# Loading the router's context a second time with its inner dimensions exchanged, in a transformer block with a routed expert layer

## The reference

```python
nx = _layer_norm(x, ln_gamma, ln_beta)
q = nx @ Wq
k = prototype_bank @ Wk            # prototype_bank is the context
v = prototype_bank @ Wv
scores = jnp.einsum('bth,bph->btp', q, k) * H ** (-0.5)
weights = jax.nn.softmax(scores, axis=-1)
evidence = jnp.einsum('btp,bph->bth', weights, v)
combined = jnp.concatenate([nx, evidence, anchor], axis=-1)
router_probs = jax.nn.softmax(combined @ router_W + router_b, axis=-1)
h = jax.nn.silu(jnp.einsum('btc,ecr->bter', combined, e_w1) + e_b1)
expert_out = jnp.einsum('bter,erh->bteh', h, e_w2) + e_b2
routed = jnp.sum(expert_out * router_probs[..., None], axis=-2)
g = jax.nn.sigmoid(jax.nn.silu(combined @ gate_w1 + gate_b1) @ gate_w2 + gate_b2)
return x + g * (routed @ out_w + out_b)
```

## Time and profile before

| | |
|---|---|
| median of 3 runs | 570.68 us (568.03 to 572.41) |
| span of the profiled execution | 569.2 us |
| TensorE busy (matmuls) | 536.2 us, 94% |
| VectorE busy | 433.4 us, 76% |
| ScalarE busy | 384.8 us, 68% |
| POOL busy | 276.2 us, 49% |

### The profile page before, as it was taken

The page is one execution under the profiler, slowest core; times in us unless marked ns, Lnnn a source line. Parts: engine busy times, 40 slices in busy tenths (PEclk is TensorE's granted clock), DMA queues, the critical chain, the costliest instruction groups (busy, mean ns, idle before and its releaser), DMA issues.

```text
span 569.2 us, 16513 instructions
## 1 busy us (share of the span) xinstructions
PE 536.2 (94%) x6209; PEld 388.2 (68%) x6209; DVE 433.4 (76%) x1271; ACT 384.8 (68%) x897; POOL 276.2 (49%) x296
## 2 busy tenths in 40 slices
PE   6988999899999999999999889998999999999995
PEld 5745666566656666666667566655888788788895
DVE  4778889788989889898877577865586686786565
ACT  6536778687777787877877575564764864864862
POOL 5637849579497787888840422224224124124100
PEclk9989999899999999999999899999999999999999
DMA  4765635534154352453410010000000000000000
GB/s 131 159 172 132 178 101 159 123 95 112 51 133 119 96 134 68 113 134 82 125 32 5 1 37 1 1 1 18 20 20 20 28 24 24 19 20 18 18 20 18
DMA packets 48716, 39.38 MB, mean 69 GB/s; under 512 B 6241, under 2 KB 48002, under 8 KB 48642
## 3 DMA queue, kind: packets, MB, share of 16 engines
q1 hardware_dynamic: 46568, 34.62, 23.2%
q10 hardware_dynamic: 2074, 3.77, 2.4%
HBM read 10.06 MB, written 2.10 MB: 21 GB/s over the span
## 4 chain that ended last, share of the span: by engine, by line
PE 64%; DVE 13%; POOL 7%; DMA 5%; issue 4%; ACT 4%; SPq 2%; ACTq 0%; DVEq 0%; POOLq 0%
PE PS L959 31%; PE PS L1837 7%; PE PS L1803 6%; PE PS L1889 4%; PE PS L995 3%; PE PS L1901 3%; DMA Qs<-MT 2%; PE PS L1821 2%; DVE NM L1617 2%; PE PS L1859 2%; PE PS L1894 2%; SPq L1347 2%; DVE r_T L934 2%; DVE r_R L937 1%; PE PS L1881 1%
## 5 line engine op out<-in xcount | busy, mean ns | idle before, releaser
L1617 DVE TENSOR_REDUCE NM<-PS 128x4 f32<-128x512 f32 x256 | 163.3, 681 | 30.1 <-PE PS L1803 29.5
L1503 ACT ACTIVATE PR<-PS 128x512 f32<-128x512 f32 x256 | 139.7, 599 | 27.2 <-PE PS L1821 26.6
L1803 PEld LDWEIGHTS PS<-Ks,Qs 64*128 64x128 bf16 x1024 | 57.7, 95 | 53.8 <-DVE NM L1617 29.6
L1803 PE MATMUL PS<-Ks,Qs 64*128 64x128 bf16 x1024 | 83.8, 219 | 5.2 <-DVE NM L1617 3.8
L1821 PE MATMUL PS<-Qs,Ks 64*128 64x128 bf16 x1024 | 84.2, 220 | 4.1 <-DMA Qs<-MT 3.5
L1837 PE MATMUL PS<-PR,Va 128*32 128x128 f32 x2048 | 84.2, 283 | 0.0
L742 ACT ACTIVATE r_HID<-PS,ANC 128x128 f32<-128x128 f32 x224 | 63.0, 381 | 19.4 <-PE PS L959 19.4
L653 POOL TENSOR_TENSOR m_veps<-m_mv,m_eps 128x4 f32<-128x4 f32 x16 | 3.6, 224 | 132.6 <-DVE m_mv L821 132.6
L1837 PEld LDWEIGHTS PS<-PR,Va 128*32 128x32 f32 x2048 | 49.0, 110 | 20.9 <-ACT PR L1503 6.5
L1821 PEld LDWEIGHTS PS<-Qs,Ks 64*128 64x128 bf16 x1024 | 57.5, 95 | 7.9 <-DMA Qs<-MT 4.0
L959 PE MATMUL PS<-r_NXS,r_WNS 128*128 128x512 f32 x168 | 53.2, 424 | 0.0
(11 more groups left out here) (201 smaller groups left out, 1121.2 us busy)
## 6 DMA issues: line engine op xcount, KB each, us to landing
Qs<-Qp SPq DMA_DIRECT2D x96, 128.0 KB
Ks<-Kp SPq DMA_DIRECT2D x90, 128.0 KB
CTXG<-in_ctx SPq DMA_DIRECT2D x8, 256.0 KB, 3.8
r_CTX<-in_ctx SPq DMA_DIRECT2D x8, 256.0 KB, 2.8
out<-X SPq DMA_DIRECT2D x8, 256.0 KB, 2.3
X<-in_x SPq DMA_DIRECT2D x7, 256.0 KB, 4.3
W<-in_weights ACTq DMA_DIRECT2D x2, 855.0 KB
Qs<-MT SPq DMA_DIRECT2D x62, 8.0 KB
```

The lines of the kernel that those rows point to most:

```text
L1503: nc.scalar.activation(PR[:, u, :], T_BANK[u % 2][:, :], ACT.Exp, scale=SCALE)\
L1617: nc.vector.tensor_reduce(out=NM[:, c.b // 2, c.second, u // 2, u % 2 * 4:u % 2 * 4 + 4, 0], in_=S_BANK[score_bank(c, u)[0]][:, :].rearran ...
L1803: last = nc.tensor.matmul(S_BANK[bank][:, j * P:(j + 1) * P], Qs[c.stack][rows, lo + j, cols], Ks[c.stack][rows, lo + j, cols], start=True ...
```

## The change

The host hands over one more array, the context with its last two dimensions exchanged. SP loads it into `CTXT` right behind the load of `CTX`, for the same group and on the same semaphore, which so counts 32 a load. As `CTXT` has one buffer, SP first waits until the keys product of the group before is done. The step `ctx_turn` goes from the lists, from TensorE and from ScalarE, and `keys` on TensorE waits for the loads and for `nx_read`. As the lists are shorter by one, the slices in `rest_of_groups` change, and with them how steps are spread there.

```diff
 ROUTER_STEPS = (
     ("probs", 0, 0), ("weigh", 1, 0),
-    ("hidden", 0, 0), ("ctx_turn", 2, 0),
+    ("hidden", 0, 0),
     ("hidden", 0, 1), ("stats", 2, 0),
...
-    for i, b in ((NG - 3, lead[0:3]), (NG - 2, lead[3:]), (NG - 1, second[:-2])):
+    for i, b in ((NG - 3, lead[0:2]), (NG - 2, lead[2:]), (NG - 1, second[:-2])):
...
-    ctx_turned = sem("ctx_turned")
-    ctx_read = sem("ctx_read")
...
                 sp.dma_start(CTX[par][:, :, :], ctxin[bass.ds(g * GB, GB)].rearrange("b p h -> p b h"))\
                     .then_inc(ctx_in[par], 16)
+                if later(g):
+                    sp.wait_ge(keys_done, g)
+                sp.dma_start(CTXT[:, :].rearrange("h (b p) -> h b p", b=GB),
+                             ctxtin[bass.ds(g * GB, GB)].rearrange("b h p -> h b p")).then_inc(ctx_in[par], 16)
...
-            elif name == "ctx_turn":
-                act.wait_ge(ctx_turned, g + 1)
-                nc.scalar.activation(CTXT[:, :], EVIDENCE_BANK[:, :], ACT.Copy).then_inc(ctx_read, 1)
...
-            if name == "ctx_turn":
-                pe.wait_ge(ctx_in[par], 16 * (pair + 1))
+            if name == "keys":
+                pe.wait_ge(ctx_in[par], 32 * (pair + 1))
                 if later(g):
                     pe.wait_ge(nx_read, g)
-                turn(EVIDENCE_BANK, lambda b: CTX[par][:, b, :]).then_inc(ctx_turned, 1)
-            elif name == "keys":
-                pe.wait_ge(ctx_read, g + 1)
                 product(EVIDENCE_BANK[:, :], A[:, :], CTXT[:, :]).then_inc(keys_done, 1)
...
+        "ctxt": np.ascontiguousarray(a["ctx_1024"].transpose(0, 2, 1)),
```

More of the change, by code:

```diff
@@ L457, in later, with mlp_and_router @@
     return not isinstance(g, int) or g > 0
-def mlp_and_router(nc, stack, X, V, ctxin, w, vec, rows1, condT, mod, gbm, half, zeros, YT, ident, PS, load_w2, out,
+def mlp_and_router(nc, stack, X, V, ctxin, ctxtin, w, vec, rows1, condT, mod, gbm, half, zeros, YT, ident, PS, load_w2, out,
                    bank_filled, bank_read, shifted_done, max_done, exp_done, o_normed, o_stored,
@@ L1127, in mlp_and_router, with build_block @@
     return sync_programs, gpsimd_programs, scalar_programs, vector_programs, tensor_programs
-def build_block(nc, xin, cond, ctxin, weights, vectors, ident_in, rowb, out):
+def build_block(nc, xin, cond, ctxin, weights, vectors, ident_in, rowb, ctxtin, out):
     stack = ExitStack()
@@ L1217, in build_block @@
         sync_programs, gpsimd_programs, scalar_programs, vector_programs, tensor_programs = mlp_and_router(
-            nc, stack, X, V, ctxin, w, vec, rows1, condT, mod, gbm, half, zeros, YT, ident, PS, load_w2, out,
+            nc, stack, X, V, ctxin, ctxtin, w, vec, rows1, condT, mod, gbm, half, zeros, YT, ident, PS, load_w2, out,
             bank_filled, bank_read, shifted_done, max_done, exp_done, o_normed, o_stored, high_ready, low_ready)
```

## The result

The changed kernel takes 562.53 us (median of 4 runs, 561.32 to 564.71), the kernel before 569.97 us in the same comparison (4 runs, 568.03 to 572.41). The ratio is 0.9884, with a 95% interval from 0.9848 to 0.9919: faster by 4.6 to 8.7 us. The forecast was 564.8 us, a ratio of 0.9897 against the 570.68 us then shown. The profiled span fell from 569.2 to 561.2 us.

A forecast was written before the change was run, and what follows sets the result against it. TensorE was taken to bound the router, busy 164.3 of 171.2 us. The terms 0.44 + 1.7 + 0.45 + 3.3 = 5.9 us, taken from 570.68, gave 564.8 us, range 562.0 to 568.0 us.

The forecast's parts named there:

- Group 0: MLP stage: four transposes leave a TensorE step and the copy is not waited for; gain 0.44 us.
- The swap on VectorE: MLP stage: router statistics come ahead of the MLP's last normalisation through the new step spread; 0, at most 1.45 us cost.
- The mixed stretch: 380 to 398 us, group 1: without the copy, keys run in TensorE's idle time, next MLP product awaits gelu; gain 1.7 us.
- Group 2: Router: only the turn's transposes are saved, as keys doesn't wait for the copy there; gain 0.45 us.
- Groups 3 to 7: Router: turn 0.45 us plus the keys product's stop 0.21 us, 0.66 us each; gain 3.3 us.
- The load: Eight added 256 KB transfers on SP, hidden by expert and hidden products, at least 12.7 us ahead of use; cost 0.
- Rival A: Waits return in mixed stretch and router, so only transposes count: 3.5 us gain, 567.2 us; chance 0.20.
- Rival B: More goes: all 6.0 us of listed TensorE waits and 8 × 0.45 us, 9.6 us, so 561.1 us; chance 0.12.
- Rival C: Slower: CTXT's load lands late, TensorE stands before keys in six groups, 1 us per us; 590.6 us at 17 us; chance 0.04.

The follow-up runs named there:

- old spread: Changed kernel with an empty step in the place of ctx_turn, so the step lists spread as in the kernel before; ratio 0.9912 to the kernel before.
- transposes back: Changed kernel with the four transposes a group back on TensorE, nobody reading them, and no copy; ratio 0.9930 to the kernel before.
- copy back: Changed kernel with ScalarE's copy back, into a spare tile, the keys product waiting for it, and no transposes; ratio 0.9973 to the kernel before.

## Why the prediction was right

The steps and what came of them, as lengths of the stretches:

- Group 0, forecast 0.44 us: 0.42 us from the first MLP product to the one at 364.03 (37.94 against 38.36 us).
- The swap on VectorE, forecast 0: 0, by the run with the old spread.
- The mixed stretch, forecast 1.7 us: 1.70 us. What is late next was the gelu, as said, 0.35 us of it.
- Group 2, forecast 0.45 us: 0.41 us (22.02 to 21.61).
- Groups 3 to 7, forecast 3.3 us: 0.67, 0.70, 0.70, 0.68 and 0.66, together 3.41 us. Hidden product 3 had 0.41 us left behind silu 0, forecast 0.44. The VectorE copy became the date of the weights' turn and was made up at the evidence product, as said.
- The load, forecast 0: 0, by the run of before with the load. For groups 2 to 7 it was issued 12.6 to 13.7 us ahead of the keys product, forecast 12.7.

The sum was 5.9 us and came out at 5.97. The median fell by 7.4 us; the 1.5 us beyond the sum are less than the spread of the timed runs (4.4 us before, 3.4 us changed), and nothing shows that they are more than scatter. Of the 2.03 us that the profiles differ ahead of the MLP, 1.4 us are a low clock in the kernel before's. Rival A's wait came (the weights' turn behind the keys copy) but cost nothing, since the next wait is longer. Rival B counted weight loads as waits and is out. Rival C's mechanism is real, one us for each us, but the load is early by 9.0 to 10.3 us. The rule of the Trainium skill (page "VectorE: DVE Perf Modes", section "The three transpose paths") on plain copies that turn by their access pattern, which it gives for a large innermost stride of the destination, did not come into play: the loads landed in 2.6 to 4.6 us, and no run here shows such a copy.

One thing in my working was right only in its sum. I priced transposes at 0.45 us and the copy's stop at 0.21 us in each of groups 3 to 7, as if one could be had without the other. The runs show that the copy's stop is 0.2 us with the transposes in front of it (before against transposes back) and 0.70 to 0.79 us without them (copy back against changed). In the mixed stretch, too, the 1.70 us are the copy's alone, as group 1's transposes cost nothing there once the copy is gone. Alone, the removal of the transposes is worth 0.6 us in the whole kernel, the removal of the copy 2.7 us, both 6.0 us.

## What to carry to other kernels

Two steps in a row on two engines, here a turn and its copy out, are priced together: if the second has a date from its own engine, taking the first away only lengthens the wait for the second. A second load of the same data in the layout that is needed was free here, on DMA engines that were busy 7% of the time and issued more than 12 us ahead of a use that it reached in 2.6 to 4.6 us; issued too late, each us of delay was paid in full. And when a step is taken out of a steady loop, its place should be used: the next wait here (0.4 us by the weight load, some 0.2 us of TensorE's time a group) went with a reordering of the lists alone.

## What the runs showed of the hardware

The granted clock of TensorE fell to its lower level (1.2 of 2.4 GHz) behind long waits in the run whose load is 4 us late; from 405 to 406 us, for one, it was 0.50. In iteration 0 TensorE was busy for 1.21 of 4 us and then went on at that level, back at 1.00 by 408 us; the windows of that run, in which 0.57 is a mean over both levels:

```profile
400.00:404.00 4.00, 1.21 (x6) 0.64 (x4) 1.24 (x8) 1.70 (x7) 1.22 (x2) 1.00 0.22 66
404.00:408.00 4.00, 3.92 (x8) 2.48 (x9) 1.74 (x5) 0.00 (x0) 0.00 (x0) 0.57 0.00 0
```

```profile
404.08 2.05 PE L960 MATMUL PS<-r_CTXT,A 128*128 128x512 f32 x2 [2.87 <-DMA r_CTXT<-in_ctxt]
```

The keys product took 2.05 us there and takes 1.02 us in the changed kernel. Iterations 0, 1 and 5 of that run lost 1.6 to 2.6 us more than iterations 2 to 4. In iteration 1 0.9 us of this are a later landing (3.7 us in place of 2.8 to 3.0), which leaves some 1.6 us for the clock in each of the three. The three falls came behind waits of 2.87, 3.92 and 3.19 us; behind those of iterations 2 to 4 (2.88, 3.05 and 3.04 us) the clock stayed at 1.00. So a wait ahead of TensorE can cost more than its length, and not each time. In the same way the kernel before lost 1.4 us at 318 us in one of its profiles and none in the other, behind a gap of 0.97 and 0.98 us. These are rows of before, then of the changed kernel, where the same work takes 320.25 − 318.07 = 2.18 us in place of 322.29 − 318.71 = 3.58 us:

```profile
318.71 2.08 PE L1901 MATMUL PS<-OgT,W 128*128 128x512 f32 x2 [0.97 <-DVE WO L796]
...
322.29 0.66 PE L1859 MATMUL PS<-ident,OTs 128*128 128x128 f32 x4
```

```profile
318.07 1.12 PE L1897 MATMUL PS<-OgT,W 128*128 128x512 f32 x2 [0.97 <-DVE WO L795]
...
320.25 0.66 PE L1855 MATMUL PS<-ident,OTs 128*128 128x128 f32 x4
```
